# Fewer, wider copies on ScalarE in the first three groups of a product-network ranking kernel

## What is computed

```python
embed = tables[jnp.arange(26)[None, :], sparse_inputs]       # 2048 x 26 x 32, from 26 tables of 12500 rows
p = jnp.einsum('bfe,bge->bfg', embed, embed)                 # products of all pairs of fields
l_z = jnp.einsum('bfe,feh->bh', embed, w_z)                  # 256 hidden
l_p = jnp.einsum('bfg,fgh->bh', p, w_p)
l_1 = relu(concatenate([l_z + l_p + l_b, dense_inputs], axis=-1))
h = relu(l_1 @ W1 + b1)                                      # 128
return sigmoid(h @ Wf + bf)
```

## Time and profile before

| what | before |
|---|---|
| median of 3 runs (lowest to highest) | 599.7 us (599.18 to 600.01) |
| span of the profiled execution | 548.8 us |
| GpSimd busy | 409.0 us, 75% of the span, 430 instructions |
| VectorE busy | 417.5 us, 76%, 250 instructions |
| ScalarE busy | 139.7 us, 25%, 333 instructions |
| TensorE busy (matmul) | 131.1 us, 24%, 204 records |
| mean granted TensorE clock | 0.683 |

### The profile page before, as it was taken

The page is one execution under the profiler, slowest core; times in us unless marked ns, Lnnn a source line. Parts: engine busy times, 40 slices in busy tenths (PEclk is TensorE's granted clock), DMA queues, the critical chain, the costliest instruction groups (busy, mean ns, idle before and its releaser), DMA issues.

```text
span 548.8 us, 1701 instructions
## 1 busy us (share of the span) xinstructions
PE 131.1 (24%) x204; PEld 48.0 (9%) x204; DVE 417.5 (76%) x250; ACT 139.7 (25%) x333; POOL 409.0 (75%) x430
## 2 busy tenths in 40 slices
PE   0000000415334100060465100051433600005067
PEld 0000000201111000020121000020110100002023
DVE  4204199998992369998996419999899547999995
ACT  0000004404551021704452010340455110250323
POOL 6777777777777777777777777777777777777792
PEclk9999999976567555585666655567665555558569
DMA  6222323122122222222112222222112222312220
GB/s 148 21 14 13 13 13 14 13 13 14 14 13 13 13 13 14 13 14 13 13 14 14 13 13 13 13 14 13 14 13 13 14 14 13 14 13 13 13 46 2
DMA packets 19640, 9.56 MB, mean 17 GB/s; under 512 B 9888, under 2 KB 19629, under 8 KB 19629
## 3 DMA queue, kind: packets, MB, share of 16 engines
q0 software_dynamic: 13312, 6.84, 22.4%
q1 hardware_dynamic: 6318, 2.63, 2.1%
HBM read 8.85 MB, written 0.01 MB: 16 GB/s over the span
## 4 chain that ended last, share of the span: by engine, by line
POOL 69%; issue 23%; DVE 6%; DMA 1%; PE 1%; ACT 0%; ACTq 0%; POOLq 0%; DVEq 0%
POOL rows L286 66%; DVE pairs L368 3%; DVE prod L348 2%; POOL prod L302 2%; POOL prod L313 1%; DMA rows<-in_L_rec_tables,which 1%; PE ps_h L643 0%; DMA raw<-in_r_sparse_inputs 0%; DVE pair_rows L404 0%; PE ps_h L680 0%; ACT scores L551 0%; PE ps_copy L692 0%; ACT hidden L537 0%; ACTq L120 0%; DVE pairs_T L395 0%
## 5 line engine op out<-in xcount | busy, mean ns | idle before, releaser
L286 POOL DMA_INDIRECT rows<-in_L_rec_tables,which x416 | 393.5, 946 | 128.4 <-issue 125.8
L348 DVE TENSOR_TENSOR prod<-ps_copy,rows 128x1664 f32<-128x1664 f32 (+12 forms) x103 | 194.2, 1910 | 16.8 <-ACT ps_copy L471 16.8
L368 DVE TENSOR_REDUCE pairs<-prod 128x76 f32<-128x2432 f32 (+13 forms) x73 | 195.3, 2680 | 0.0
L626 PE MATMUL ps_h<-field_rows,wz 128*128 128x512 f32 x96 | 59.4, 784 | 290.3 <-ACT field_rows L482 285.4
L379 DVE STREAM_TRANSPOSE rows_T<-rows 128x512 f32<-128x512 f32 (+1 forms) x28 | 18.6, 663 | 98.1 <-DMA rows<-in_L_rec_tables,which 90.7
L471 ACT COPY ps_copy<-rows 128x128 f32<-128x128 f32 (+2 forms) x63 | 21.2, 336 | 273.3 <-DMA rows<-in_L_rec_tables,which 273.0
L643 PE MATMUL ps_h<-pair_rows,w_pair 96*128 96x512 f32 (+2 forms) x64 | 50.2, 943 | 100.3 <-ACT pair_rows L505 84.4
L482 ACT COPY field_rows<-rows_T 32x512 f32<-32x512 f32 (+1 forms) x112 | 58.7, 524 | 34.9 <-DVE rows_T L379 33.4
L626 PEld LDWEIGHTS ps_h<-field_rows,wz 128*128 128x128 f32 x96 | 23.8, 258 | 328.0 <-issue 292.1
L505 ACT COPY pair_rows<-pairs_T 32x256 f32<-32x256 f32 (+1 forms) x96 | 33.5, 349 | 63.1 <-DVE pairs_T L391 61.9
L643 PEld LDWEIGHTS ps_h<-pair_rows,w_pair 96*128 96x128 f32 (+2 forms) x64 | 17.7, 296 | 130.4 <-ACT pair_rows L505 71.9
(11 more groups left out here) (37 smaller groups left out, 31.7 us busy)
## 6 DMA issues: line engine op xcount, KB each, us to landing
rows<-in_L_rec_tables,which POOLq DMA_INDIRECT x416, 3.4
wz<-in_L_rec_w_z SPq DMA_DIRECT2D x1, 768.0 KB, 5.8
field_rows<-rows_T SPq DMA_DIRECT2D x16, 32.0 KB, 1.9
w_pair<-in_w_low SPq DMA_DIRECT2D x1, 288.0 KB, 5.4
w_back<-in_w_high SPq DMA_DIRECT2D x1, 288.0 KB, 5.7
raw<-in_r_sparse_inputs SPq DMA_DIRECT2D x1, 156.0 KB, 2.2
w<-in_L_rec_W SPq DMA_DIRECT2D x1, 128.0 KB
dense_in<-in_r_dense_inputs SPq DMA_DIRECT2D x1, 104.0 KB, 3.2
```

The costliest lines, as they stand in the source:

```text
L286: nc.gpsimd.indirect_dma_start(rows[:, r % 2, f, k, :], None, table_rows, bass.IndirectOffsetOnAxis(ap=which[:, t, f:f + 1], axis=0),).the ...
L348: ins = nc.vector.tensor_tensor(products(r, s)[:, 0:tiles, at:at + g + 1, :], own.broadcast_to([P, tiles, g + 1, E]), rows[:, r % 2, 0:g + ...
L368: nc.vector.tensor_reduce(pairs[:, 0:tiles, first:end], products(r, s)[:, 0:tiles, :, :], AX.X, ALU.add)\
L626: ins = nc.tensor.matmul(ps_h0[:, h, :], wz[:, j, h * P:(h + 1) * P], field_rows[:, j, :, :, :].rearrange("p q t b -> p (q t b)"), start=( ...
```

## The change

In the first three groups (`ROUNDS - 1`):

- Fields 12 to 25 are copied to PSUM by twos, 10 units a group instead of 15. The stages of VectorE stay one field each.
- All six whole chunks are one move (16 copies of 768 elements), and all three pair blocks are one (12 copies of 384). The pair blocks are transposed by one instruction, when the last of them is added up.
- All of these copies stand behind the copy of fields 24 and 25: rows, pairs, then the last chunk. TensorE does all chunks, then the three pair blocks, then the dense columns and the tail.

As `turn_rows` goes by units, chunk 4 is transposed ahead of field 18's product instead of field 19's, chunk 5 ahead of field 22's instead of 23's. The last group keeps its moves and its order; the numbers that semaphores are waited on for are counted anew, since the groups now differ.

```diff
-UNITS = [[(0, 4), (4, 8), (8, 12), (12, 14), (14, 16)] + [(f, f + 1) for f in range(16, 26)]] * (GROUPS - 1) + [FINE]
+UNITS = [[(0, 4), (4, 8), (8, 12)] + [(f, f + 2) for f in range(12, 26, 2)]] * (GROUPS - 1) + [FINE]
...
-    MOVES = [(0, 4), (4, MOVED), (MOVED, CH)]
-    NM = len(MOVES)
+    MOVES = [[(0, MOVED), (MOVED, CH)]] * (ROUNDS - 1) + [[(0, 4), (4, MOVED), (MOVED, CH)]]
+    MOVES_BEFORE = [sum(len(moves) for moves in MOVES[:r]) for r in range(ROUNDS + 1)]
...
-    PAIR_MOVES = [(0, 2), (2, 3), (TAIL, TAIL + 1)]
-    NPM = len(PAIR_MOVES)
+    PAIR_MOVES = [[(0, TAIL), (TAIL, TAIL + 1)]] * (ROUNDS - 1) + [[(0, 2), (2, 3), (TAIL, TAIL + 1)]]
+    PAIR_MOVES_BEFORE = [sum(len(moves) for moves in PAIR_MOVES[:r]) for r in range(ROUNDS + 1)]
...
+    def laid_after(r, j):
+        return MOVES_BEFORE[r] + move_of(r, j) + 1
+
+    def pairs_laid_after(r, c):
+        return PAIR_MOVES_BEFORE[r] + pair_move_of(r, c) + 1
...
                 if r:
-                    dve.wait_ge(rows_laid, NM * (r - 1) + move_of(j) + 1)
+                    dve.wait_ge(rows_laid, laid_after(r - 1, j))
...
                         make_scores(r - 1)
-                    if first in (14, 16, 17, 18):
-                        lay_rows(r, 0, (14, 16, 17, 18).index(first))
-                    if 20 <= first < 23:
-                        lay_pairs(r, 0, first - 20)
-                    if first == 23:
-                        lay_rows(r, SP_MOVE, 0)
                     if first == 24:
-                        lay_rows(r, SP_MOVE, 1)
-                for q in range(2, QUADS):
-                    lay_rows(r, SP_MOVE, q)
+                        for q in range(QUADS):
+                            lay_rows(r, 0, q)
                 for u in range(PLACES):
-                    lay_pairs(r, 1, u)
+                    lay_pairs(r, 0, u)
                 lay_last_rows(r)
...
             for r in range(ROUNDS):
-                for j in range(*MOVES[0]):
+                for j in range(*MOVES[r][0]):
                     sum_lz(r, j)
-                for c in range(*PAIR_MOVES[0]):
+                for c in range(*PAIR_MOVES[r][0]):
                     sum_lp(r, c)
                 sum_dense(r)
-                for j in range(*MOVES[1]):
-                    sum_lz(r, j)
-                for c in range(*PAIR_MOVES[1]):
-                    sum_lp(r, c)
+                if r == ROUNDS - 1:
+                    for j in range(*MOVES[r][SP_MOVE]):
+                        sum_lz(r, j)
+                    for c in range(*PAIR_MOVES[r][1]):
+                        sum_lp(r, c)
                 sum_lp(r, TAIL)
```

More of the change, by code:

```diff
@@ L97, in unit_of, with move_of, pair_move_of @@
         return next(u for u, (first, end) in enumerate(UNITS[r]) if first <= f < end)
-    def move_of(j):
-        return next(m for m, (first, end) in enumerate(MOVES) if first <= j < end)
-    def pair_move_of(c):
-        return next(m for m, (first, end) in enumerate(PAIR_MOVES) if first <= c < end)
+    def move_of(r, j):
+        return next(m for m, (first, end) in enumerate(MOVES[r]) if first <= j < end)
+    def pair_move_of(r, c):
+        return next(m for m, (first, end) in enumerate(PAIR_MOVES[r]) if first <= c < end)
+    def laid_after(r, j):
+        return MOVES_BEFORE[r] + move_of(r, j) + 1
+    def pairs_laid_after(r, c):
+        return PAIR_MOVES_BEFORE[r] + pair_move_of(r, c) + 1
     def block_rows(c):
@@ L206, in pnn_kernel, with field_end @@
         MLP_LOADS = 6
-        PAIR_END = [BLOCK * PAIR_MOVES[0][1], BLOCK * PAIR_MOVES[1][1], NP]
-        FIELD_END = [next(g for g in range(NF) if pairs_before(g + 1) >= end) for end in PAIR_END]
+        def field_end(r, m):
+            end = min(BLOCK * PAIR_MOVES[r][m][1], NP)
+            return next(g for g in range(NF) if pairs_before(g + 1) >= end)
         def ps_copy_bank(c):
@@ L242, in _ @@
             r = ROUNDS - 1
-            first, end = MOVES[SP_MOVE]
+            first, end = MOVES[r][SP_MOVE]
             sp.wait_ge(rows_turned, CH * r + end)
@@ L364, in add_up @@
                 if r and s == 0:
[L366 removed]
+                    dve.wait_ge(pairs_turned, PAIR_MOVES_BEFORE[r])
                     dve.wait_ge(tail_turned, r)
@@ L383, in turn_pairs @@
             def turn_pairs(r, m):
-                first, end = PAIR_MOVES[m]
-                dve.wait_ge(summed, NS * r + stage_of(r, FIELD_END[m]) + 1)
-                if r == ROUNDS - 1 and m == NPM - 1:
+                first, end = PAIR_MOVES[r][m]
+                dve.wait_ge(summed, NS * r + stage_of(r, field_end(r, m)) + 1)
+                if r == ROUNDS - 1 and first == TAIL:
                     dve.wait_ge(pool_summed, 1)
                 if r:
-                    dve.wait_ge(pairs_laid, NPM * (r - 1) + m + 1)
+                    dve.wait_ge(pairs_laid, pairs_laid_after(r - 1, first))
                 if first < TAIL:
@@ L450, in _ @@
                         add_up(r, s - 1)
-                        for m in range(NPM):
-                            if stage_of(r, FIELD_END[m]) == s - 1:
+                        for m in range(len(PAIR_MOVES[r])):
+                            if stage_of(r, field_end(r, m)) == s - 1:
                                 turn_pairs(r, m)
@@ L474, in lay_rows @@
             def lay_rows(r, m, q):
-                first, end = MOVES[m]
+                first, end = MOVES[r][m]
                 if q == 0:
@@ L497, in lay_pairs @@
             def lay_pairs(r, m, u):
-                first, end = PAIR_MOVES[m]
+                first, end = PAIR_MOVES[r][m]
                 if u == 0:
-                    act.wait_ge(pairs_turned, NPM * r + m + 1)
+                    act.wait_ge(pairs_turned, PAIR_MOVES_BEFORE[r] + m + 1)
                     if r:
```

11 lines of the change are left out of this document (5 added, 6 removed).

## The result

The changed kernel takes 693.3 us (four runs, 693.28 to 693.44), the kernel before 599.6 beside it: ratio 1.1566 [1.1549, 1.1582]. It is slower by 93.7 us, where no change was forecast.

A forecast was written before the change was run, and what follows sets the result against it. GpSimd's indirect gathers, one every 1.25 us, were taken to bound the kernel. Gathers, hand-over and tail each added 0, so span 548.8 + 50.9 around it = 599.7 us, no change; range 598.8 to 600.7.

The forecast's parts named there:

- 50.9 us lie around the span: Median time 599.7 less profiled span 548.8; 50.9 us was added to any span to get a time.
- TensorE's burst: All 42 matmul records of a group, now after the row copies and ahead of hidden0: 20.9 us, upper end 39.7.
- The first rival: TensorE stays at half clock through its long burst, hidden0 20.7 us late: +6.1 us, 605.8; chance 5%.
- 14.6 us of slack: In group four, how late VectorE's fields 4/5 may start before the end moves, against 2 us of expected lateness.
- break-even of 0.80 us a record: TensorE's 42 records must take over 33.5 us, 0.80 each, before their lateness lengthens the kernel.
- ScalarE's terms: Lay-out copies per changed group: 16 row copies 13.4 us, 12 pair copies 6.2; busy time falls 18 us, none on the chain.
- the overlap of 93 ns: Skill figure for back-to-back ScalarE copies: 16 row copies in 11.8 us instead of 13.4; the profile row was preferred.
- The hand-over: Group three to four: pair copies from 410.6, hidden0 ends 432.4, fields 4/5 2 us late; 0 at the end.
- That rival: Copying fields by twos starves VectorE inside groups, up to 5.0 us a pair: +10 us, 609.8; chance 2%.
- Gathers 0, hand-over 0, tail 0: Sum of the change's effects on the span: none, leaving 548.8 us and a time of 599.7 us.

The follow-up runs named there:

- without gathers: Changed kernel with groups two to four loading fixed table rows by plain SyncE DMAs instead of indirect gathers; 488.2 us, ratio 0.8158.
- with memsets: Kernel before plus 78 one-column GpSimd memsets, one behind each field's gathers in the first three groups; 609.8 us, but 550.96 on the sixth chip.
- the kernel with idle-time copies: Changed kernel plus 20 one-column ScalarE copies a group ahead of hidden0; 550.94 us on the sixth chip, ratio 1.1572 on another.
- the thinned one: Kernel before with TensorE's sum_lz and sum_lp counting once a move, 5 increments a group instead of 10; ratio 0.9997.
- the one with hidden0 late: Changed kernel with hidden0, hidden1 and scores moved behind fields 18, 20 and 22 of the next group; 598.9 us, ratio 1.0003.
- the kernel with tiny matmuls: Changed kernel plus two tiny zero-weight matmuls behind each half chunk in the first three groups, 48 more TensorE instructions a group; 775.8 us.

## Why the prediction was wrong

**The mechanism.** In the condition of the timed runs, beside the gathers, what TensorE's instructions release comes in turns of 1.40 us an instruction once the first 18 or so have passed, however small they are (91.8 us for 84; slopes of 1.396 and 1.40 in both directions; 21.0 without gathers). ScalarE's short copies start 1.40 us apart. The kernel before spreads TensorE's instructions over the group, in bursts at 103.2, 129.9, 155.4, 171.4 and 189.6, and its first hidden0 starts at 194.9 (168.8 in the recorded page). The change puts all 84 behind the last row copy, at 151.0. ScalarE waits for them ahead of the copy of fields 4 to 7, VectorE behind that copy, and the next burst can't start before VectorE and ScalarE have gone through a group: 91.8 + 88.6 = 180.4 us a cycle, longer than the gathers. The sum comes out: 151.0 + 180.4 + 180.7 + 74.6 (the third burst, 512.1 to 586.7, shorter because the gathers end at about 560) + 104.4 = 691.1. The prediction's steps, one by one:

- **"50.9 us lie around the span", taken as a constant: the step that failed.** It is 2.1 to 2.2 us in every execution of before and after that has both span and time (1.8 with memsets and without gathers). The gap said that the profiled execution (548.8) was not of the kind that was timed (599.7), and I added it instead of asking where 47 us of such a run go. The Trainium skill bears on this ("Runtime: NRT & Kernel Launch", section "The ~15µs preamble/postamble breakdown"): it calls the difference between a profile's total and the execution time independent of the kernel, about 6 us. There the profile's total is the longer of the two; here the time is, by 2.1 us, so the figure is not the same. That the gap hardly depends on the kernel is borne out here, and by that the 50.9 would have been noticed.
- **TensorE's burst, 20.9 us (bounded by 39.7): the term that was mis-sized.** It measured 91.8 us from first matmul to hidden0, 2.19 a record. The price per record was read from the recorded page, and for the matmuls themselves it is right everywhere: 21.5 us in the kernel with idle-time copies in that condition, 21.0 without gathers, and 22.7 us of busy time in after. What the sum lacked is a wait between the end of a matmul and the arrival of what it releases. In the other condition that wait sets the length, and neither bound holds, since both count a record's own duration.
- **The first rival** had the right place: a longer burst, hidden0 late, 14.6 us of slack behind it. Its break-even of 0.80 us a record was passed far. Its cause, the granted clock, was not the one: in after the clock was 1.00 (2.4 GHz) from 151 to 171 us, while 38 of the 42 records ran, and even 42 records at half clock, 39.7 us, would be less than half of 91.8. Its chance, 5%, was read from rows of the wrong condition.
- **ScalarE's terms hold in the profile's condition.** 16 copies of 768 in 13.43 us (13.4 forecast), 828 ns each; 12 of 384 in 6.24 (6.2). In after the 12 need 12.55 us, from 150.90 to 163.45. Of the overlap of 93 ns between neighbours that the Trainium skill gives ("ScalarE: Activation LUTs", section "What ACT_TABLE_LOAD costs"), weighed in the prediction at 11.8 us, nothing shows in these copies: the row was the right choice.
- **The hand-over holds in the profile's condition.** Pair copies from 410.77 (410.6 forecast), group four's first copy at 419.51 (419.2), hidden0's end at 433.03 (432.4), the product of fields 4/5 at 433.34 against 430.84, 2.5 us late (2 forecast), and the wait of 1.99 us ahead of field 21 is gone. The slack took it: 550.94 against 550.99.
- **Pairing does not starve VectorE**: it costs 1.3 us (0.7 to 2.0) in the condition of the timed runs. That rival's mechanism is out.
- **"Gathers 0, hand-over 0, tail 0"** is right for the gathers even in after: the last one starts at 558.9, before at 559.9. The chain left them and went over to the hand-over.

**What is open.** What makes the condition. It went with the chip, or with the time at which its runs were made, which were never parted; five of the six chips with experiments had it, and the recorded page of before did not, while its timed runs did. In it, the traces hold far fewer records of semaphore increments: 1378 for the kernel before, where the recorded page has 7869 (7202 of them of DMA landings). From 160 to 500 us every trace of before or after from the five chips holds 484 to 488 of them, one per 0.70 us, which is half a turn; the recorded page and the two traces from the sixth chip hold 4573 to 4583, and the run without gathers 1200. So the turns go together with a trace that keeps fewer records, at an even pace, and in the recorded page most of these records are landings of gathers, some 16 for each. The Trainium skill has a candidate ("NOTIFIC — the notification-queue block", section "Overflow: three behaviours, one of which stalls the engine"): in one of three settings a full notification queue holds back whoever reports to it. It would fit turns that do not depend on the instruction's size and the even 0.70 us. That the queue was full, or that it holds the engines back, no run here shows. Every timed execution of the experiments stands on record with a span of its own, so something was recorded in all of them; whether the changed kernel is slower than the one before when nothing is recorded is open too. Also open: why the kernel before, the thinned one and the one with hidden0 late all stay at 598 to 599, beyond the fact that their gathers run to 560 and the tail takes 36 us instead of 26. No version here beats both kernels.

## What to carry to other kernels

Compare the profile's span with the timed runs before any sum is made: a gap far above that of other runs (50.9 us here, where 2.2 is usual) is not overhead but a profile of another condition, and every duration and every slack read from it is in doubt. Where short instructions stand at even distances with nothing to wait for (1.40 us here), count instructions and not only microseconds: spread them, and put nothing that others need behind the end of a long burst on another engine. The changed kernel with its hidden layer 12 to 16 fields later ran level with before on the same burst, so a consumer's place in its engine's order is worth as much as the burst's length.

## What the runs showed of the hardware that was not expected

- A turn of 1.40 us an instruction on TensorE and ScalarE, beside indirect gathers, on five chips of six; for a matmul of one column as for one of 512, for a copy of 0.19 us as for one of 0.51. On TensorE it holds back first what is released and only after some 90 instructions the starts (166.9 in the kernel with tiny matmuls); on ScalarE it holds back the starts. VectorE's instructions are mostly longer than 1.40 us, and none of these runs tests it. TensorE's weight loads count as instructions of their own (2.80 us for record and load).
- Increments of semaphores cost nothing in it: hidden0 moved by under 0.5 us between 3 and 16 a group.
- The gathers themselves fall into the same step in stretches. GpSimd in the kernel before, profiled again:

```profile
301.40 0.94 POOL L286 DMA_INDIRECT rows<-in_L_rec_tables,which  x1 [0.30 <-issue]
302.65 0.95 POOL L286 DMA_INDIRECT rows<-in_L_rec_tables,which  x1 [0.30 <-issue]
...
309.95 1.09 POOL L286 DMA_INDIRECT rows<-in_L_rec_tables,which  x1 [0.30 <-issue]
311.35 1.09 POOL L286 DMA_INDIRECT rows<-in_L_rec_tables,which  x1 [0.30 <-issue]
```

From 1.25 us apart to 1.40, in the duration and not in the idle ahead of it. Over all gathers the busy time is 31.8 us more than in the recorded page and the idle 5.6, which makes the 37 us up to the last gather. What starts it isn't shown.
